# New stage orders for all five engines of a fused quantised-FFN and expert-routing kernel; first x loaded in four pieces; filler matmuls taken out

## The reference

```python
def _smooth_quant_linear(x, w):
    s = jnp.sqrt(max(amax_x, EPS) / max(amax_w, EPS))      # per column, amax over rows
    xs, ws = x / s, w * s
    x_scale, w_scale = rowmax(|xs|) / 127, rowmax(|ws|) / 127
    x_q, w_q = round(xs / x_scale), round(ws / w_scale)
    return x_q @ w_q.T * x_scale * w_scale.T

def _expert_forward(xe, guw, dw):                          # for each of the 4 batches
    gate, up = split(_smooth_quant_linear(xe, guw), 2)
    return _smooth_quant_linear(silu(gate) * up, dw)

x = x + vmap(_expert_forward)(layernorm(x), fside, ctx)
# then, for every token of y = layernorm(x): softmax over y @ router_w, the best 2 of 8 experts,
# and the weighted sum of silu(y @ gate_proj[e]) * (y @ up_proj[e]) @ down_proj[e] over those 2
x = x + moe(layernorm(x), router_w, gate_proj, up_proj, down_proj)
```

## Time and profile before

| | us |
|---|---|
| runs shown | 409.56, 410.62, 411.88 |
| median | 410.62 |
| profiled execution, its own time | 408.86 |
| its span, first to last instruction | 406.9 |

### The profile page before, as it was taken

How to read it: one execution, slowest core, us unless ns; L and a number is a source line. 1 busy time by engine, 2 the same in 40 slices (tenths; PEclk the granted TensorE clock), 3 DMA queues, 4 the chain that set the end, 5 groups by cost and what they waited for, 6 DMA issues and landing times.

```text
span 406.9 us, 6243 instructions
## 1 busy us (share of the span) xinstructions
PE 343.2 (84%) x1860; PEld 204.4 (50%) x1860; DVE 233.6 (57%) x512; ACT 206.3 (51%) x386; POOL 244.3 (60%) x264
## 2 busy tenths in 40 slices
PE   5767867876987886889989988999999999999960
PEld 3435425564656753467545634555555555545420
DVE  1675888799698999875855674333333333333310
ACT  1439669968776657151942545344444343434330
POOL 5374896999577965266237314546667666666340
PEclk9898989998699599895999999999999999999995
DMA  6840934739546562203471373655876567766552
GB/s 207 278 163 16 345 156 146 268 102 363 155 157 217 197 207 67 89 26 87 103 226 27 53 234 105 120 107 88 151 123 118 98 111 131 116 138 108 82 70 26
DMA packets 26590, 56.77 MB, mean 140 GB/s; under 512 B 2560, under 2 KB 12800, under 8 KB 24512
## 3 DMA queue, kind: packets, MB, share of 16 engines
q0 software_dynamic: 8736, 20.45, 27.9%
q1 hardware_dynamic: 17824, 35.93, 25.3%
HBM read 37.50 MB, written 18.87 MB: 139 GB/s over the span
## 4 chain that ended last, share of the span: by engine, by line
PE 48%; DVE 24%; POOL 8%; issue 7%; ACT 6%; DMA 4%; POOLq 0%; DVEq 0%; SPq 0%; ACTq 0%
PE bank_h L1255 19%; PE bank_q L1276 9%; DVE rmax L725 5%; PE bank_q L1127 4%; PE bank_t L1240 3%; DVE amax L695 3%; PE bank_t L1127 3%; PE bank_q L1178 2%; DVE xn L737 2%; DVE onehot L842 2%; PE bank_r L1212 2%; PE bank_h L1155 2%; DMA w_in<-tokens,gather_at 2%; PE bank_r L1266 1%; DVE packed L849 1%
## 5 line engine op out<-in xcount | busy, mean ns | idle before, releaser
L1255 PE MATMUL bank_h<-gu_hi,xT 128*128 x312 | 104.6, 381 | 1.4 <-DVE xT L928 1.2
L1255 PE MATMUL bank_h<-gu_lo,xT 128*128 x156 | 59.6, 382 | 0.0
L928 DVE SCALAR_TENSOR_TENSOR xT<-bank_t,xT 128x512 f16<-128x512 f32 x39 | 26.8, 690 | 53.9 <-ACT xT L1056 53.7
L1276 PE MATMUL bank_q<-dn_hi,aT 128*128 x156 | 52.8, 379 | 2.3 <-DVE aT L946 2.0
L1255 PEld LDWEIGHTS bank_h<-gu_hi,xT 128*128 128x128 f16 x312 | 30.7, 98 | 31.4 <-issue 3.0
L639 POOL DMA_INDIRECT w_in<-tokens,gather_at x30 | 29.9, 997 | 20.4 <-DVE gather_at L913 10.3
L567 POOL TENSOR_TENSOR gu_lo<-stage,gu_hi 128x1024 bf16<-128x1024 f32 x16 | 34.6, 2172 | 12.2 <-ACT gu_hi L1013 12.1
L936 DVE SCALAR_TENSOR_TENSOR gated<-bank_h,gated 128x256 f32<-128x256 f32 x39 | 16.5, 423 | 33.1 <-ACT gated L1063 33.1
L695 DVE TENSOR_REDUCE amax<-bank_t 128x1 f32<-128x512 f32 x48 | 31.0, 684 | 6.7 <-PE bank_t L1127 6.6
L660 POOL DMA_INDIRECT out<-h,scatter_at x17 | 26.9, 1584 | 13.0 <-DMA out<-h,scatter_at 4.7
L1063 ACT ACTIVATE gated<-bank_h 128x256 f32<-128x256 f32 x39 | 15.0, 384 | 37.3 <-PE bank_h L1255 37.3
(11 more groups left out here) (192 smaller groups left out, 741.0 us busy)
## 6 DMA issues: line engine op xcount, KB each, us to landing
x_in<-in_x SPq DMA_DIRECT2D x4, 1024.0 KB, 5.2
w_in<-in_fside_BxS2xS SPq DMA_DIRECT2D x4, 1024.0 KB, 5.3
stage<-in_L_ffn_gate_proj SPq DMA_DIRECT2D x8, 512.0 KB, 5.1
stage<-in_L_ffn_up_proj SPq DMA_DIRECT2D x8, 512.0 KB, 4.1
stage<-in_L_ffn_down_proj SPq DMA_DIRECT2D x8, 512.0 KB, 4.6
x<-in_x SPq DMA_DIRECT2D x4, 1024.0 KB, 6.7
out<-x SPq DMA_DIRECT2D x4, 1024.0 KB, 7.5
tokens<-xn SPq DMA_DIRECT2D x4, 1024.0 KB, 6.3
```

The costliest lines, as they stand in the source:

```text
L928: dve.scalar_tensor_tensor(out=xT[i % 2][:, 1].rearrange("p c t -> p (c t)"), in0=bank, scalar=X_SCALE, in1=xT[i % 2][:, 0].rearrange("p c ...
L1255: ins = pe.matmul(bank, xT[i % 2][:, part, c], rhs[:, cols], start=(c == 0 and m == 0), stop=(c == C - 1 and m == 2))
L1276: ins = pe.matmul(bank, aT[i % 2][:, part, c], rhs[:, cols], start=(c == 0 and n == 0), stop=(c == FC - 1 and n == 2))
```

## The change

- All five order tables are written anew (the diff shows two of their lines).
- `FILLERS`, `keep_busy`, the tile `nothing` and its memset are gone; PE no longer waits for the three constants that only the fillers used. With them, small waits move: "product" waits for its sources before it takes a bank, and so on.
- Batch 0's x is loaded by four transfers of 256 KB, one per quarter of the rows of a partition, each with its own semaphore; "moments 1 0" waits for each piece. The other batches are loaded as they were.

```diff
 SP_ORDER = in_order(
-    "load x 0, load w1 0, load expert 0, load w2 0, load expert 1, load x 1, load expert 2, load expert 3, "
+    "load x 0, load w1 0, load expert 0, load expert 1, load w2 0, load expert 2, load expert 3, load x 1, "
...
-FILLERS = {
-    ("w1 columns", 0): 14, ("rows 1", 0): 6, ("w1 scale row", 0): 14, ("rows 2 inverse", 0): 16,
-    ("a transposed", 1): 6, ("place", 0): 13, ("sort step", 0): 3, ("sort step", 1): 8, ("sort step", 2): 16,
-    ("sort step", 3): 4,
-}
...
             def load_x(b):
                 if b > 0:
                     sp.wait_ge(sem("xn_ready"), upto(b - 1, J))
-                sp.dma_start(x_in[:], x_dram[b]).then_inc(sem("x_in"), 16)
+                    sp.dma_start(x_in[:], x_dram[b]).then_inc(sem("x_in"), 16)
+                else:
+                    for j in range(J):
+                        sp.dma_start(x_in[:, j], x_dram[b][:, j]).then_inc(sem(f"x_piece{j}"), 16)
...
                 for j in range(J):
-                    if j < per_batch:
-                        dve.wait_ge(ready, upto(b, per_batch, j) * (16 if per_batch == 1 else 1))
+                    if which == 0 and b == 0:
+                        dve.wait_ge(sem(f"x_piece{j}"), 16)
...
             def product(stage, lhs, rhs, sources, b):
+                for source in sources:
+                    ring_q.emptied(pe, source, lhs.shape[1] - 1, b)
                 for j in range(J):
                     bank = ring_h.fill(pe, stage, j, b)
-                    if j == 0:
-                        keep_busy(bank, stage, b)
-                        for source in sources:
-                            ring_q.emptied(pe, source, lhs.shape[1] - 1, b)
...
-                    for _ in range(FILLERS.get(("sort step", step), 0)):
-                        if n == 0:
-                            pe.matmul(bank, below[:], number[:].rearrange("p l j -> p (l j)"), start=True, stop=True)
-                        else:
-                            pe.matmul(bank[:, 0:3 * P].rearrange("p (v l) -> p v l", v=3), nothing[:],
-                                      number[:, 0:3 * P // J].rearrange("p (v l) j -> p v (l j)", v=3), start=False, stop=False)
```

More of the change, by code:

```diff
@@ L211, in block_kernel @@
         onesb = sb("onesb", [P, P], BF16)
-        nothing = sb("nothing", [P, P], BF16)
         power = sb("power", [P, 2, C], F32)
@@ L1103, in _ @@
         def _(pe):
[L1104 to L1106 removed]
+            pe.wait_ge(sem("constants"), 4)
             pe.wait_ge(sem("mean_made"), 1)
@@ L1111, in _ @@
             ins.then_inc(sem("means"), 1)
-            def keep_busy(bank, stage, b):
-                for _ in range(FILLERS.get((stage, b), 0)):
-                    pe.matmul(bank, below[:], number[:].rearrange("p l j -> p (l j)"), start=True, stop=True)
             def transposed(ring, stage, src, n, ready, count, b):
+                pe.wait_ge(ready, count * (b + 1))
                 for c in range(n):
                     bank = ring.fill(pe, stage, c, b)
-                    if c == 0:
-                        keep_busy(bank, stage, b)
-                        pe.wait_ge(ready, count * (b + 1))
                     for j in range(J):
@@ L1128, in transposed, with as_row @@
                     ins.then_inc(ring.filled, 1)
-            def as_row(ring, stage, b, columns, fillers, ready, count):
+            def as_row(ring, stage, b, columns):
                 bank = ring.fill(pe, stage, 0, b)
-                keep_busy(bank, fillers, b)
-                pe.wait_ge(ready, count)
                 for c in range(columns.shape[1]):
@@ L1161, in tokens @@
                     n = 2 * pair + j
+                    pe.wait_ge(sem("x1_ready"), n + 1)
                     bank = ring_q.fill(pe, "tokens", j, pair)
-                    if j == 0:
-                        keep_busy(bank, "tokens", pair)
-                    pe.wait_ge(sem("x1_ready"), n + 1)
                     for c in range(C):
@@ L1172, in router @@
                 pe.wait_ge(sem("centred"), 1)
+                ring_q.emptied(pe, "tokens", 1, pair)
                 bank = ring_q.fill(pe, "scores", 0, pair)
-                keep_busy(bank, "scores", pair)
-                ring_q.emptied(pe, "tokens", 1, pair)
                 for j in range(2):
@@ L1187, in rank @@
                 rank = bank[:, 0:(m + 1) * E].rearrange("p (t e) -> p t e", e=E)
-                keep_busy(bank, "place", g)
                 pe.wait_ge(sem("mask_ready"), g + 1)
```

35 lines of the change are left out of this document (18 added, 17 removed), and 97 rows, old and new, of tables (ACT_ORDER, DVE_ORDER, PE_ORDER, POOL_ORDER).

## The result

The changed kernel takes 417.42 us (median of 4 executions, 416.37 to 418.11), the kernel before 411.25 us beside it (409.56 to 411.9): a ratio of 1.0152, 95% interval 1.0117 to 1.0187. In a later series, 1.0166 (1.0136 to 1.0197). It is slower by 6.2 us in the first series and by 6.5 us in the second. The prediction (407.3, range 400 to 414) was wrong in sign, and the time lies above its range. The ratios leave out the few executions that were slowed as a whole, and the profiles of experiments 1 and 12 are of such slowed ones, so only distances within them are read.

What follows compares the result with a forecast made beforehand. It took DVE to bound 73.6 to 150.8 us and PE the late tiles from 254.3 us; seven terms summed to -3.3 us, 408.86 to 405.6, or 407.3 us on the median's footing, range 400 to 414.

Steps and rivals of the forecast that it cites:

- Step 1: Opening, to x columns 0: x in pieces starts statistics sooner, partly lost to cold w1 transposes; -0.7 us.
- Step 2: Batch 0, to a columns 0: weights first makes DVE wait longer, about 6.1 us, before w1 columns 1; +2.4 us.
- step 3: Product 1 1: without 16 fillers PE transposes xq and wq cold, partly hidden behind ACT; +0.6 us.
- Step 4: Up to place 0: DVE stalls fall from 10.1 to 6.8 us, with 0.6 us more work; -2.7 us.
- Step 5: Place 0's end to a scales 3: product 1 3 is already done, 20.4 against 24.0 us; -3.6 us.
- Step 6: Early tiles to first late tile: sorting stages come sooner, x low 9 waits for its gather; -1.3 us.
- Step 7: Clock elsewhere: the other fillers were on no path, but PE runs some stages cold without them; +2.0 us.
- rival B: Routing gets cheap: DVE's one-hots no longer stand behind POOL's lows, winning 6 us; 401 us, chance 0.22.
- C: Batch 0's delay stays: PE's w1 columns wait for loads, DVE stalls over 10 us; 413.7 us, chance 0.16.
- E: No effect: the early tiles eat the head start at a scales 3; 410.5 us, chance 0.16.
- D: TensorE stays at 1.2 GHz through part 1, transposes not counting for the clock; 420 us, chance 0.06.

Runs made afterwards that it cites:

- experiment 1: The changed kernel with the matmuls on constants put back at the old stages and counts; 1.0029 of the kernel before.
- experiment 12: The changed kernel with TensorE's x low 9 moved back behind take y 8, ScalarE's order unchanged; 1.0030 of the kernel before.
- experiment 11: The changed kernel with matmuls on constants put back and ScalarE's x high 9 ahead of take y 7; 0.9981 of the kernel before.
- experiment 6: Experiment 4's kernel with all engines' old orders for batch 0, up to batch 1's transposes; 1.0028 of the kernel before.
- experiment 3: The kernel before with only batch 0's x loaded in four transfers; 0.9969 of the kernel before.
- experiment 2: The changed kernel with the old five order tables: x in four transfers, no matmuls on constants; 0.9999 of the kernel before.
- experiment 8: Experiment 4's kernel with GpSimd's low 19 waiting until DVE has written all four packed tables of place 0; 1.0282 of the kernel before.
- experiment 9: Experiment 3's kernel with GpSimd's low 20 waiting until DVE has written gather_at for the early tiles; 1.0046 of the kernel before.
- experiment 4: The changed kernel with ScalarE's x high 9 put ahead of its take y 7, nothing else moved; 1.0036 of the kernel before.
- experiment 13: The changed kernel with GpSimd's scatter 4 moved ahead of its gather 9, nothing else moved; 1.0111 of the kernel before.

## Why the prediction was wrong

The terms of the sum, against the two profiles of the changed kernel, each as the difference of a stretch to the profile before (us):

| stretch, by its end | predicted | first profile | second profile |
|---|---|---|---|
| 1. x columns 0 | -0.7 | -0.5 | -0.5 |
| 2. a columns 0 | +2.4 | +3.7 | +2.2 |
| 3. product 1 1 | +0.6 | +0.4 | +0.4 |
| 4. start of place 0 | -2.7 | -0.4 | -0.5 |
| place 0 itself | not in the sum | +2.8 | +2.9 |
| 5. a scales 3 | -3.6 | -2.7 | -1.6 |
| 6. first late tile | -1.3 | +4.7 | +2.9 |
| the late tiles | 0 | +1.6 | -0.1 |
| 7. clock elsewhere | +2.0 | in the rows above | in the rows above |
| sum | -3.3 | +9.5 | +5.8 |

**Steps 1 to 3 held.** Step 1's loss by cold transposes shows when the matmuls on constants are put back: x columns 0 then ends at 19.42 us (experiment 11) for 20.33. The stall ahead of w1 columns 1 came where it was forecast, at 6.7 us in the first profile and 5.7 in the second, for 6.1. It wasn't w1's load that ended last before it, as the step has it, but TensorE's x transposed 0, which ran until 42.8 us in the first profile, with w1 columns 1 right behind it. Step 2's cause was also sized well for the wrong reason in part: experiment 6 shows that, without matmuls on constants, the old order of batch 0 ends only 0.2 us sooner. The delay is at least as much their absence as weights first: in the old orders their absence alone moves a columns 0 from 51.43 to 52.34 us (experiments 3 and 2).

**Step 4 failed in its stalls.** I counted 6.8 us of idle time on DVE; it is 76.71 - 64.95 = 11.8. The walk with old durations found root 1 2 and rows 1 2 (1.7 and 1.3 us) but the rest, 4.2 us by my count, came to 8.8, of which 5.7 are waits for product 1 and product 2. What saved the stretch is something that I had not counted: choose 0, with 4.94 us for 7.13, met fewer lows.

**Place 0 was no term at all.** I wrote that the new order again has low 19 to 22 and gate times up 3 beside it, used that against rival B, and then left its length at the old 18.2 us. It took 21.0, 0.6 us more on top of what choose 0 had gained. That the price moves and doesn't vanish is the point: in experiment 8 place 0 gave 8.8 us and list 0 took 7.5 of them, in experiment 9 place 0 gave 2.6 and indices 0 took 3.6. Rival B was right about the mechanism and its price per low, about 2 us. Its condition, that the new order leaves place 0 alone, did not come, and experiments 8 and 9, which made it come in whole or in part, got slower.

**Step 5 held in direction**, with 2.7 and 1.6 us for 3.6. ScalarE's long wait behind the sorting didn't go, though ("ACT has no 10 us wait"): it stands 15.72 us for tokens 4. No run tests what that wait costs.

**Step 6 is the step that failed most**, with +4.7 and +2.9 us for -1.3. It says "x low 9 waits some 2 us for its gather instead" and stops there. The wait was 0.77 us. What I did not do is what step 6 needed: read ScalarE's end of that order. x high 9 is appended behind take y 7 and 8 by the code, and TensorE's table now has x low 9 ahead of them. Before, both engines had it last. Experiments 4 and 12 show that this pair costs 1.3%, 5.5 us, in an otherwise unchanged kernel. The profiles show where 3.6 of them are: between gather 9 and the first late tile there are 10.51 us with the pair and 6.93 without. Where take y 8 comes on time, in experiments 1 and 13, it is 8.88 and 8.87 us, so the pair by itself makes 1.9 us and the late take y 8, which x high 9 must wait for in that order, the other 1.6.

Mending the pair doesn't bring step 6's -1.3 us either: experiment 4's stretch is 62.52 us, +1.2. What is left there goes with TensorE's clock. It stood at 1.00 from 191.7 us on before, and fell twice in this stretch in the first profile and once in the second. The same 316 matmuls kept it busy 58.1 us for 55.8, and 58.1 in experiment 4 too (in the second profile 55.9, but with seven of them missing from the trace). The clock fell twice in experiments 1 and 11 too, with the matmuls on constants back, so their absence doesn't explain it. That points at the new order of the early tiles, but no run tests it.

**Step 7 failed in a sentence, not in its size.** "The trace has them on no path, so taking them out saves nothing" was right for the old orders, where their absence costs 0.3%, and +2.0 us is near the 0.5% of the new ones with the join in order, two differences that are hardly clear of noise. In the changed kernel they are worth 1.4%, which is. Of that the profile shows 1.6 us at the join, by the take y 8 that isn't late; where the rest lies stays open. The step also had no term for the late tiles. In the first profile the first of them ran at 0.50, behind 3.3 us in which TensorE stood. In the second it stood 3.5 us there and ran at 1.00, so the wait alone doesn't settle it:

```profile
263.30:266.50 3.20, 3.20 (x9) 1.27 (x8) 0.00 (x0) 0.00 (x0) 1.58 (x1) 0.50 0.43 60
```

**The range.** The bounds of the seven terms are not centred on the terms: their middles add up to -0.35 us, not -3.3. Half their widths, squared and added, give +-7.7 us, not +-5. From the prediction's own bounds the range would have been 402.5 to 418.0 us.

**The rivals.** C's sign came true (stalls of 11.8 us for its 10), but not its mechanism: DVE's waits for w1 and x columns in that stretch are 0.5 us in all. That its price, 413.7, is near the kernel with the join mended and without the matmuls (412.7 by 1.0036 of 411.25) is luck. E did not come: there was no head start at a scales 3 that could be eaten (196.20 and 195.99 us for 192.93). D did not come: the clock was 0.87 between 77 and 154 us. Behind a stretch with float32 transposes alone it even rose (TensorE's timeline, then the busy times on either side):

```profile
30.02 1.11 PE L1123 MATMUL bank_r<-identf,scale 128*128 128x128 f32 x4 [5.89 <-DVE inv L728]
30.93 1.92 PE L1116 MATMUL bank_t<-identf,w_in 128*128 128x128 f32 x8
32.63 2.44 PE L1116 MATMUL bank_q<-identf,w_in 128*128 128x128 f32 x12
```
```profile
20.90:34.40 13.50, 6.34 (x28) 5.55 (x28) 9.68 (x15) 6.13 (x9) 11.53 (x7) 0.50 0.43 149
34.60:37.80 3.20, 1.13 (x8) 0.65 (x7) 2.31 (x10) 2.93 (x6) 1.70 (x4) 1.00 0.42 127
```

As far as they start before 34.4 us, these are, with eight transposes from 22.16 us on, the 28 matmuls of the first stretch. From 10 to 34.5 us this kernel has neither products nor matmuls on constants, so these rows speak more plainly than the earlier trace rows did. The Trainium skill (TensorE: Matmul & The Clock Gate, "Part 4: PE-mode transpose") has it that transposes don't count as activity for the clock; for the float32 transposes of this kernel the measurement decides against it.

What is shown: the join's pair of orders (4, 12), the price of a low beside DVE and that it moves (8, 9), the small worth of batch 0's order without the matmuls (6), the worth of the matmuls on constants in the changed kernel (1). What is only read from the traces: how the pair's cost splits at the join, and the cold stretches among the early tiles as the rest of step 6. What stays open: why take y 8 comes late, and what the matmuls on constants have to do with it.

## What to carry to other kernels

When an order is made anew, check every hand-over between two engines at the seams, above all where one side comes from a table and the other is appended by code: one stage that is first on one engine and last on the next cost more here than anything that these runs can show the new order to have won. A contention between two engines is a term of the sum wherever both work; moving the work moves the price, and by the rows it falls only if the operations that it meets are of the kind that doesn't wait, which no run here tried. Before holding work back, ask what else its end releases (here staging buffers, and through them loads).
